# Three score banks and two maxima banks in an attention and mixture-of-experts kernel

## What is computed

```python
q = _split(lora_linear(x, Wq, bq, Bq, Aq))
k = _split(lora_linear(x, Wk, bk, Bk, Ak))
v = _split(lora_linear(x, Wv, bv, Bv, Av))
scores = jnp.einsum('bhqd,bhkd->bhqk', q, k) * SCALE
attn = jax.nn.softmax(scores, axis=-1)
out = jnp.einsum('bhqk,bhkd->bhqd', attn, v)
```

## Time and profile before

| | us |
|---|---|
| median of 3 runs (lowest, highest) | 1094.25 (1091.41, 1097.25) |
| the profiled execution: its time | 1093.02 |
| the profiled execution: span from first to last instruction | 1091.4 |
| PE busy | 1041.3 (95%) |
| DVE, ACT, POOL busy | 724.1, 557.3, 540.3 |
| prologue (to the first score of half 0) | 113.0 |
| halves 0 to 15 | 513 |
| output projection, experts, layer norm | 465 |
| transfers into `Qs`, 128 KB each: median from issue to landing | 2.3 |

### The profile page before, as it was taken

One profiled execution on the slowest core, in us unless ns is written; L12 is line 12 of the kernel. 1 busy time (PEld: TensorE's weight loads), 2 busy tenths in 40 slices (PEclk: granted clock), 3 DMA queues, 4 the chain that ended last, 5 costly groups with the idle time before them and its releaser, 6 DMA issues.

```text
span 1091.4 us, 16143 instructions
## 1 busy us (share of the span) xinstructions
PE 1041.3 (95%) x5586; PEld 726.8 (67%) x5586; DVE 724.1 (66%) x1194; ACT 557.3 (51%) x978; POOL 540.3 (50%) x294
## 2 busy tenths in 40 slices
PE   6999999999999999999999988968999999999996
PEld 5777555455555545556445567756899999998884
DVE  5549878878687787888887576512476666664154
ACT  4311556656466565666665654411355656664116
POOL 2100788889878898788889830370000000003600
PEclk9999999999999999999999999989999999999998
DMA  7964342724337142332641492350277777765704
GB/s 265 306 180 136 83 112 56 174 65 95 78 78 175 49 111 55 78 97 51 169 154 63 124 287 72 117 139 18 70 211 214 215 239 229 222 201 125 112 1 154
DMA packets 163765, 146.79 MB, mean 134 GB/s; under 512 B 42529, under 2 KB 126753, under 8 KB 163440
## 3 DMA queue, kind: packets, MB, share of 16 engines
q1 hardware_dynamic: 157040, 129.97, 42.8%
q0 software_dynamic: 6656, 15.93, 5.3%
HBM read 85.75 MB, written 35.67 MB: 111 GB/s over the span
## 4 chain that ended last, share of the span: by engine, by line
PE 78%; DVE 7%; DMA 4%; issue 4%; ACT 4%; SPq 2%; ACTq 0%; DVEq 0%
PE bank L812 16%; PE bank L964 13%; PE bank L977 11%; PE bank L912 11%; PE bank L900 8%; PE bank L1109 8%; PE bank L1022 4%; PE bank L872 3%; PE bank L989 3%; DMA raw<-in_L_ffn_W_dram 2%; DVE w2lo L1735 1%; DVE mx L1606 1%; DMA bcol<-in_L_attn_bk_dram 1%; PE bank L819 1%; DVE sa L1742 1%
## 5 line engine op out<-in xcount | busy, mean ns | idle before, releaser
L1336 ACT ACTIVATE prob<-bank 128x512 f32<-128x512 f32 x512 | 289.9, 597 | 194.3 <-PE bank L964 186.3
L1606 DVE TENSOR_REDUCE mx<-bank 128x1 f32<-128x512 f32 x512 | 324.9, 680 | 81.5 <-PE bank L912 78.6
L740 POOL TENSOR_TENSOR psum<-psum,prob 128x1024 f32<-128x1024 f32 x156 | 366.8, 2388 | 1.0 <-ACT prob L1336 1.0
L964 PE MATMUL bank<-Qs,Ks 97*128 97x512 f32 x512 | 209.0, 424 | 0.9 <-DMA Qs<-mrow 0.9
L912 PE MATMUL bank<-Ks,Qs 96*128 96x512 f32 x512 | 184.6, 405 | 3.8 <-DVE mx L1606 1.3
L964 PEld LDWEIGHTS bank<-Qs,Ks 97*128 97x128 f32 x512 | 94.3, 188 | 106.3 <-ACT prob L1336 74.3
L791 POOL DMA_DIRECT2D oe_d<-oe_sb x16 | 8.8, 548 | 248.8 <-ACT oe_sb L1474 247.8
L977 PE MATMUL bank<-prob,V 128*32 128x512 f32 x1024 | 131.4, 602 | 0.0
L912 PEld LDWEIGHTS bank<-Ks,Qs 96*128 96x128 f32 x512 | 97.2, 190 | 50.2 <-DVE mx L1606 21.8
L740 POOL TENSOR_TENSOR psum<-prob,prob 128x1024 f32<-128x1024 f32 x32 | 76.0, 2394 | 67.8 <-ACT prob L1336 37.8
L900 PE MATMUL bank<-xThi,Wsl 128*128 128x512 f32 x256 | 99.6, 400 | 3.8 <-DMA bcol<-in_L_attn_bk_dram 3.1
(11 more groups left out here) (251 smaller groups left out, 2067.9 us busy)
## 6 DMA issues: line engine op xcount, KB each, us to landing
raw<-in_L_ffn_W_dram SPq DMA_DIRECT2D x120, 256.0 KB
Ks<-plane_khi SPq DMA_DIRECT2D x64, 128.0 KB, 2.7
Qs<-plane_qhi SPq DMA_DIRECT2D x64, 128.0 KB, 2.3
raw<-in_L_ffn_sw_dram SPq DMA_DIRECT2D x30, 256.0 KB
xin<-in_L_attn_x_dram SPq DMA_DIRECT2D x16, 256.0 KB, 5.0
v_d<-v_sb POOLq DMA_DIRECT2D x16, 256.0 KB, 3.9
Wsl<-wt_d SPq DMA_DIRECT2D x16, 256.0 KB, 4.7
Ks<-plane_klo SPq DMA_DIRECT2D x32, 128.0 KB, 2.5
```

What stands on the lines that cost most here:

```text
L740: po.tensor_tensor(psum[:, pr], (prob[0] if kc == 1 else psum)[:, pr], prob[kc % RING][:, pr], ALU.add).then_inc(sem("sum_done"), 1)
L964: nc.tensor.matmul(score_at(v, i), Ks[v.b][0:97, hh, kc * P:(kc + 1) * P], Qs[v.b][0:97, hh, v.hf * HALF:(v.hf + 1) * HALF], start=True, s ...
L1336: ACTV(prob[kc % RING][:, hh, :], score_at(v, i), ACT.Exp, scale=SCALE).then_inc(sem("exp_done"), 1)
L1606: ins = RED(mx[(hf + ahead) % 2][:, 4 * hh + qt, part:part + 1], src, AX.X, ALU.max)
```

## The change

The bank counts are swapped: maxima get banks 0 and 1, scores get banks 2, 3 and 4. `EVEN` and `ODD` are new tables with the same letters in other places. `PRO_ORDER` and the three `LAST_` tables stay as they are, and now work on the new banks. No instruction is added or taken away.

```diff
-WORK, SCORE = 3, 2
+WORK, SCORE = 2, 3
@@
-EVEN = ("mmm vle imm m p m p m mopmmp m "
-        "mmq v mm m v - imm im v - "
-        "mvr mi mm m v m mn v m mm "
-        "hv mmz")
-ODD = ("m vm m lom m mv mm m em mm "
-       "pi pmm p mmm i qpm mvvv - mmm p "
-       "ip m mppm rqvvimn p m p mh mm v "
-       "mp mzqp")
+EVEN = "mmlm m - m pm mpm mpm meim pmq i vmom vm m - m m m - m mvm m ivm ri vm m v nm mh - mzv m mv"
+ODD = "mmlm m vm mo - - mmv mm em m ippm m pm mi pimq - mi vvnv m mppphm mpmq vr - mp mp mm pm - mpm zm - mqvv"
```

## The result

| | us |
|---|---|
| before: median of 4 runs (lowest, highest) | 1095.03 (1091.41, 1097.25) |
| changed: median of 4 runs (lowest, highest) | 1118.91 (1118.34, 1121.06) |
| changed: span of the profiled execution | 1119.4 |
| ratio, with 95% interval | 1.0215 (1.0188 to 1.0243) |

The change costs 23.9 us, 2.2%. "The kernel before" is always the denominator unless another is named.

A forecast was written before the change was run, and what follows sets the result against it. PE was taken to bound the halves and DVE the prologue. Terms 7.3 + 1.7 + 5.4 + 1.5 + 3.3 + 0.6 = 19.8 on the profiled 1093.0 gave 1112.8, forecast as 1112 us, range 1100 to 1121.

The forecast's parts named there:

- halves 13 and 14: Old tables on two maxima banks: bursts wait 4.0 us in half 13, 3.7 in half 14; +7.3 us after 0.4 back.
- prologue, opening of half 0, its 21st maximum: Bank waits of 0.9 us in the prologue and 0.8 at half 0's opening, plus 1.5 at half 0's 21st maximum.
- even halves 2 to 12: Each takes 31.15 us against 30.2, through lone groups, small waits and the 21st maximum; +5.4 us for six.
- odd halves and slab: Six odd halves wait for tiles before the 5th maximum, +3.3 us; halves 5 and 9 for the weight slab, +0.6.
- The turn-round of one bank: One maxima bank can take a new maximum every 1.17 us; with two banks that binds the third maximum.
- The wait behind three operations on a row tile in half 14: Longest burst wait of half 14, where an earlier maximum's reduction stands behind those operations: 1.3 us.
- The opening: Half 0's first maximum needs the bank that the prologue's last one filled: 0.8 us.
- The path from the last projection pass to the first issue: Even halves, ahead of the 21st maximum: about 1.9 us instead of 3.2, as `q` stands directly behind the projection.
- `l` and `e` that now stand alone: Even halves have ten lone groups of small-column matmuls, 29.95 us without any wait, against 29.2 before.
- The clock: Rival: the new waits make the clock fall in six more places, 1.5 us each, giving 1122 us; chance 0.09.
- The wait in front of the 5th maximum: Odd halves: tiles land 0.35 us too late, 0.55 with slower landings; +3.3 us for six.
- The slab: At the first `p` of halves 5 and 9, PE waits 0.3 us more for the weight slab in each; +0.6.

The follow-up runs named there:

- tables_only: The changed kernel's tables on the old bank counts (three for maxima, two for scores); ratio 1.0284 to the kernel before.
- banks_only: The kernel before with the bank counts alone swapped (two for maxima, three for scores), old tables; ratio 1.0689.
- last_spaced: The changed kernel with the tables of halves 13 and 14 rewritten to space the maxima; ratio 1.0175 to the kernel before.
- slab_again: Repeat, without further edit, of the kernel before with three of six weight slab issues moved ahead of `mrow` in the even half; ratio 0.9981.
- slab_early: The kernel before with three of the six weight slab issues moved ahead of `mrow` in the even half; ratio 0.9978.
- after_again: The changed kernel run once more with no edit, on another chip; ratio 1.0222 to the kernel before.
- tiles_in_time: The changed kernel with the projection's end two slots earlier in `EVEN`, 5th and 6th maximum of `ODD` one slot later; ratio 1.0144 to the kernel before.

## Why the prediction was right, and where it was not

Forecast 1112 us, 1.7% slower; measured 1118.9, 2.2%. The direction, the places and the mechanism were right: maxima wait for two banks where the tables are old, and for tiles where they are new. The terms, against the two profiles of the changed kernel:

| term | forecast | first profile | second profile |
|---|---|---|---|
| halves 13 and 14 | 7.3 | 8.3 | 8.3 |
| prologue, opening of half 0, its 21st maximum | 3.2 | 4.7 | 4.6 |
| even halves 2 to 12 | 5.4 | 7.5 | 4.3 |
| odd halves and slab | 3.9 | 4.4 | 3.2 |
| ahead of the first maximum; behind half 14 | 0 | 3.2 | (another chip) |
| sum | 19.8 | 28.1 | 20.4 |

The profile of the changed kernel is of its longest run (1121.06), that of before is near its shortest (1093.02), which is why 28 stands here against 23.9 of the medians. The second profile is of that kernel's fastest execution, 7 us under its median, so its 20.4, close to the forecast 19.8, is the lower edge and not the typical loss.

*Halves 13 and 14.* The turn-round of one bank was forecast as 1.17 and is 1.18; `tables_only` shows that the term is all of it. Mis-sized was the end of a wait: I had the next matmul start 0.23 behind the one that was held, and it starts 0.34 behind. For fourteen bursts that makes 14 x 0.11 = 1.5 more; 1.0 more was measured. The wait behind three operations on a row tile in half 14, forecast as 1.3, is there:

```profile
604.84 0.50 PE L906 MATMUL bank<-Ks,Qs 96*128 96x512 f32 x1 [1.14 <-DVE mx L1600]
```

The Trainium skill (Perfetto Trace Analysis, Optimizing Tensor Performance, Matmuls) asks that matmul groups rotate through banks; by it alone this term was 0. The runs differ with it: two banks in rotation cost 8.3 us here and three cost none.

*Prologue and half 0.* The opening waits 0.77, then 0.55 (0.8 forecast in one piece):

```profile
117.90 0.73 PE L906 MATMUL bank<-Ks,Qs 96*128 96x512 f32 x2 [0.77 <-DVE mx L1600]
...
119.18 0.50 PE L906 MATMUL bank<-Ks,Qs 96*128 96x512 f32 x1 [0.55 <-DVE mx L1600]
```

The prologue itself lost 1.5 instead of 0.9: where a maximum that was held is followed by another on its bank, the 0.1 comes on top, and the bank turns round in 1.28.

*Even halves.* Forecast 31.15 each, and 30.91 to 30.96 in eleven of the twelve that the two profiles have, half 4's 34.06 being the other. The path from the last projection pass to the first issue was forecast at 1.9 and is 261.20 - 259.55 = 1.65, so the 21st maximum waits 0.37 instead of 0.75. The largest part of this term, 0.8 us in each half for `l` and `e` that now stand alone, was not tested by itself.

*The clock.* This rival came true in half 4: a wait of 1.7 us was followed by slow matmuls, the regular ones were not. The twelve waits for banks in halves 13 and 14, 0.3 to 1.14 us each, left the clock at 1.00 in both windows. The Trainium skill (TensorE: Matmul & The Clock Gate, A second HAM failure mode) has the clock go back and forth with such waits between groups; these two halves do not show it. But other runs do. In `banks_only`, with its 99 waits, the clock falls to 0.50 in halves 0, 6 and 8, in half 6 behind waits of 0.31 and 0.65 us, and half 0 of `last_spaced` takes 32.3 instead of 30.9 because the clock falls behind the same two waits of 0.78 and 0.55 that left it at 1.00 in the changed kernel:

```profile
117.70:121.00 3.30, 3.30 (x8) 2.58 (x9) 2.35 (x4) 1.78 (x4) 0.00 (x0) 0.50 0.80 180
```

*Odd halves.* The wait in front of the 5th maximum was put down to 16 regular issues and a slow landing, 0.55 in each half. In half 7 it is 0.2, in halves 3 and 11 0.9 to 1.2. The step was right on average, but that is luck in part, as it had the wrong cause for half of it: the slow issue, which my rows of before did not show because the tables there had slack.

*The slab.* Halves 5 and 9 lost 0.8 and 0.6 in one profile and -0.4 and 0.3 in the other (0.3 each forecast, with the odd halves' own 0.55). The difference in half 5 is the clock: it fell behind the wait of 2.52 us in the first profile and stayed at 1.00 behind one of 2.70 in the second.

## What to carry to other kernels

Count for each PSUM bank how long it is held, from the matmul's start to the end of what reads it, and compare that with the distance of the matmuls that share it, at every place that uses the pool: also in tables that the change does not touch. A bank taken from one pool has to be paid by the order of work, and if that order was written for the other split, neither half of the change may be judged alone. A chain of DMA issues with no slack ahead of an in-order engine is hit by whatever makes one issue late; give it a slot or two more than its regular length. That a bank's hold follows the length of the reduction is read from rows; no run changed that length.

## What the hardware showed that I had not expected

- A matmul that was held by a semaphore costs 0.11 us more than its wait: 0.50 in its row and 0.34 to the next start, against 0.40 and 0.23.
- The instruction queue fetches 16 KB about every 25 us in the halves (39 times in all), and the fetches go with PE's stream. Of 50 SP issues that met one, 35 took 1.3 to 2.2 us instead of 0.6. Forty more waits in SP's stream did not move them.
- A fulfilled wait costs PE 0.05 us (100 of them, 5.3 us) and SP 0.03 (40, 1.2 us) where nothing hides them. Two share an instruction in the trace: 50 on PE, 0.11 us apart, and 20 on SP, 0.06 apart.
- The length of the last wait does not say whether the clock falls. It stood at 0.58 for 4 us behind the wait of 1.70 in half 4, and at 0.59 for 3 us behind the one of 1.54 in half 6 of `slab_again` (below). It fell behind 0.91 in half 0 of `slab_early` and behind 0.65 in half 6 of `banks_only`, and it stayed at 1.00 behind 1.14 in half 14 of the changed kernel, and behind 2.70 in half 5 of `after_again` and 2.60 in half 5 of `tiles_in_time`:

```profile
330.90:334.00 3.10, 3.10 (x12) 1.11 (x13) 0.97 (x2) 0.05 (x1) 3.10 (x3) 0.59 0.00 0
```
